# A focus attention kernel: later key groups four steps apart, their operations in another order on three engines

## The reference

```python
x = x + 0.5 * time_mix_ffn(layernorm(x))
x = x + causal_attention(layernorm(x))          # 16 heads of 8
x = x + 0.5 * time_mix_ffn(layernorm(x))
x = x + 0.5 * mixture(layernorm(x))             # 8 experts, top 2, hidden 256
x = x + focus(layernorm(x))
x = x + 0.5 * mixture(layernorm(x))
```

```python
kp = k_full @ lk_w.T + lk_b;  vp = v_full @ lv_w.T + lv_b
sk = ln(kp, lnd_w)                              # per head of 8
for i in range(3):
    sq = ln(qcur @ lq_w.T + lq_b, lnc_w) * rsqrt(temp)
    out = softmax(sq @ sk.T * INV_SQRT) @ vp
    diff = mean(abs(out - prev))                # decides on convergence
    qcur = qcur + out
output = out @ Wo.T + bo
```

## Time and profile before

| | |
|---|---|
| median of 3 runs | 1460.45 us (1457.98 to 1462.42) |
| the profiled execution | 1457.98 us, span 1456.2 us |
| PE busy | 1306.4 us (90%) |
| DVE busy | 1009.1 us (69%) |
| ACT busy | 869.7 us (60%) |
| POOL busy | 529.0 us (36%) |

### The profile page before, as it was taken

How to read it: one execution, slowest core, us unless ns; L and a number is a source line. 1 busy time by engine, 2 the same in 40 slices (tenths; PEclk the granted TensorE clock), 3 DMA queues, 4 the chain that set the end, 5 groups by cost and what they waited for, 6 DMA issues and landing times. The chain is left out here.

```text
span 1456.2 us, 36645 instructions
## 1 busy us (share of the span) xinstructions
PE 1306.4 (90%) x11651; PEld 920.2 (63%) x11651; DVE 1009.1 (69%) x3275; ACT 869.7 (60%) x1613; POOL 529.0 (36%) x818
## 2 busy tenths in 40 slices
PE   3699989989859999999999998999899998899998
PEld 2566766666636787776555555665555555577876
DVE  3688898898737873787677666767767666587444
ACT  3477777777524444434677777877677676333453
POOL 6366666665320320412233333343322321012444
PEclk9799999999969999999999999999999999899999
DMA  5322322322121012103445454555444442001332
GB/s 137 95 75 58 86 69 61 86 77 67 34 78 55 16 48 79 37 14 82 120 126 126 126 130 117 132 137 130 115 115 113 120 120 65 2 16 44 100 108 80
DMA packets 81070, 123.64 MB, mean 85 GB/s; under 512 B 10124, under 2 KB 64676, under 8 KB 71722
## 3 DMA queue, kind: packets, MB, share of 16 engines
q1 hardware_dynamic: 77866, 115.71, 30.7%
q0 software_dynamic: 3072, 6.30, 1.5%
HBM read 88.28 MB, written 33.56 MB: 84 GB/s over the span
## 5 line engine op out<-in xcount | busy, mean ns | idle before, releaser
L1417 ACT ACTIVATE e_buf<-ps_q 128x1024 f32<-128x1024 f32 x192 | 196.8, 1025 | 105.0 <-PE ps_q L2142 103.3
L2153 PE MATMUL ps_o<-e_buf,v_st 128*32 128x256 f32 x3072 | 209.5, 391 | 5.0 <-POOL v_st L1022 4.2
L1417 ACT ACTIVATE e_buf<-ps_k 128x1024 f32<-128x1024 f32 x192 | 196.0, 1021 | 19.6 <-PE ps_k L2142 19.5
L2003 PEld LDWEIGHTS ps_o<-w,e_buf 128*128 128x128 f32 x1280 | 152.2, 193 | 13.1 <-issue 12.0
L2003 PE MATMUL ps_o<-w,e_buf 128*128 128x128 f32 x1280 | 158.5, 277 | 0.0
L2591 DVE TENSOR_REDUCE mx<-ps_q 128x3 f32<-128x384 f32 x256 | 130.1, 548 | 27.4 <-PE ps_q L1707 26.8
L2142 PE MATMUL ps_q<-q_st,k_st 73*128 73x256 bf16 x768 | 118.5, 277 | 16.4 <-DMA q_st<-scr_q 13.2
L1234 ACT ACTIVATE e_buf<-ps_k 128x768 f32<-128x768 f32 x128 | 103.3, 807 | 47.3 <-PE ps_k L1718 45.4
L2153 PEld LDWEIGHTS ps_o<-e_buf,v_st 128*32 128x32 f32 x3072 | 81.3, 110 | 75.9 <-issue 36.8
L2142 PEld LDWEIGHTS ps_q<-q_st,k_st 73*128 73x128 bf16 x768 | 61.2, 98 | 96.8 <-issue 47.4
L3116 DVE COPY o_sb<-ps_o 128x256 f32<-128x256 f32 x192 | 80.0, 418 | 59.6 <-PE ps_o L2153 55.9
(11 more groups left out here) (403 smaller groups left out, 3063.5 us busy)
## 6 DMA issues: line engine op xcount, KB each, us to landing
q_st<-scr_q SPq DMA_DIRECT2D x64, 576.0 KB
k_st<-scr_k SPq DMA_DIRECT2D x192, 192.0 KB
scr_q<-parts SPq DMA_DIRECT2D x64, 192.0 KB, 2.9
scr_k<-parts SPq DMA_DIRECT2D x72, 64.0 KB
slots_in<-heads_out SPq DMA_DIRECT2D x3, 1536.0 KB
slots_out<-heads_out SPq DMA_DIRECT2D x18, 256.0 KB, 2.0
heads_out<-slots_in SPq DMA_DIRECT2D x15, 256.0 KB
out_dram<-x SPq DMA_DIRECT2D x8, 256.0 KB
```

The costliest lines, as they stand in the source:

```text
L1417: act.activation(e_buf[g % 2][:, hp * 2 % HG:hp * 2 % HG + 2, :], (ps_q, ps_k)[hp % 2][:, :, :], ACT.Exp).then_inc(sem("fast_exp"), 1)
L2003: last = mm(ps_o[:, e % 2, t * P:(t + 1) * P], h_sb[e % 2][:, f, t * P:(t + 1) * P], w2[:, e * NF + f, :], start=f == 0, stop=f == NF - 1)
L2153: last = mm(ps_o[VW * j:VW * j + VW, g % 2, 0:T], v_st[p][:, kt, HG * g + j, :], e_buf[g % 2][:, j, kt * T:(kt + 1) * T], start=kt == 0, s ...
```

## The change

The five pieces of a group start every four steps instead of every three. On TensorE the early value group of a late step is gone (order as in a plain step), and key_tokens is issued at hp 6 instead of at the end of the step. On VectorE key_queries and key_values come behind front_deviations and key_stats1, and key_norm2 comes behind the second evacuation. On SyncE the wait for the stores of the last group comes before fast_operands. The wait for the constants moves from inside the first mixture to ahead of it, on TensorE and VectorE.

```diff
-            return [(g, b - 3 * i) for i, g in enumerate(range(KEYS_LATE + 1, NG)) if 0 <= b - 3 * i <= 4]
+            return [(g, b - 4 * i) for i, g in enumerate(range(KEYS_LATE + 1, NG)) if 0 <= b - 4 * i <= 4]
...
 # SyncE
                         for g in late:
                             key_parts(g, late_parts)
+                            if g == NG - 1:
+                                sp.wait_ge(sem("K_out"), (g + 2) * 48 * GB)
                         if ahead:
                             fast_operands(*ahead, p, half + 1)
                         for g in late:
-                            sp.wait_ge(sem("K_out"), (g + 2) * 48 * GB)
+                            if g < NG - 1:
+                                sp.wait_ge(sem("K_out"), (g + 2) * 48 * GB)
...
 # TensorE, hp 3
-                                if late:
-                                    fast_values(n, p, 0)
                                 for g, step in late:
                                     if step == 1:
                                         pe.wait_ge(sem("K_hi"), g + 1)
...
                                 if not first:
                                     back_tokens(n - 1, b - 1, it, 0)
-                                if not late:
-                                    fast_values(n, p, 0)
+                                fast_values(n, p, 0)
...
 # TensorE, hp 6
-                                    if step in (2, 3):
+                                    if step in (1, 2, 3):
                                         pe.wait_ge(sem("fast_o_read"), (n - 1 + B) * NT + NT + 1)
+                                    if step == 1:
+                                        key_tokens(g)
...
 # TensorE, hp 7
                                 fast_values(n, p, 2)
-                                for g, step in late:
-                                    if step == 1:
-                                        pe.wait_ge(sem("fast_o_read"), (n - 1 + B) * NT + NT + 1)
-                                        key_tokens(g)
...
 # TensorE and VectorE, first mixture
-                    pe.wait_ge(sem("consts"), CONSTS + 8)
                     positions(k)
...
+            pe.wait_ge(sem("consts"), CONSTS + 8)
             for g in range(AHEAD):
                 mixture(g, g % 2, 0, True, more=lambda g, e: ahead(0, g, e))
...
 # VectorE, a step
                             evacuate_group(n - 1, NGV - 1)
-                        for g, step in late:
-                            if step == 2:
-                                key_queries(g)
-                            if step == 3:
-                                key_values(g)
                         if ahead:
                             front_deviations(ahead[0])
                         for g, step in late:
                             if step == 0:
                                 key_stats1(g)
+                        for g, step in late:
+                            if step == 2:
+                                key_queries(g)
+                        for g, step in late:
+                            if step == 3:
+                                key_values(g)
...
-                        for g, step in late:
-                            if step == 1:
-                                key_norm2(g)
                         evacuate_group(n, 1)
...
                                 key_norm1(g)
+                        for g, step in late:
+                            if step == 1:
+                                key_norm2(g)
```

More of the change, by code:

```diff
@@ L3580, in ahead @@
                 if (g, e) == (1, 1):
-                    dve.wait_ge(sem("consts"), CONSTS + 8)
                     tile_experts(k)
@@ L3636, in weigh_tiles @@
                 quad_out(CHUNKS[k][-1], QUADS - 1)
+            dve.wait_ge(sem("consts"), CONSTS + 8)
             for g in range(AHEAD):
```

## The result

The changed kernel took 1481.99 us as a median of four runs (1478.0 to 1485.28), the kernel before 1461.43 beside it, also of four. The ratio on record, 1.0165 with a 95% interval of 1.0131 to 1.02, is taken over all 34 executions of the changed kernel on record, and 1.65% of 1461 is 24 us; the two medians of four alone differ by 20.6. The direction was as forecast, the size not: 20.6 to 24 us slower where the forecast's sum had 12.0, and 1482 lies above the range's 1479. The profiled execution took 1485.11 us, 27 more than the one before.

What follows compares the result with a forecast made beforehand. The prediction took TensorE, busy 90% of the span, as the bound. Its terms summed to +12.0 us, giving 1470.0 from the profiled run and 1472.5 from the median, taken as 1471; range 1465 to 1477, widened to 1463 to 1479.

Steps and rivals of the forecast that it cites:

- Part 1: Groups start at steps 0, 4, 8: no work goes away, and moving piece 0 off the 15 us steps buys nothing.
- Part 2: TensorE in late steps, wait and transposes before the value product: −0.45 us where the wait is already met (pieces 0, 1, 4).
- Part 3: VectorE's order in pieces 2 and 3: TensorE waits uncovered; +1.6 us per piece 2 (+4.8), piece 3 at 15.4 (+1.1).
- Part 4: Piece 1, key_norm2 behind the second evacuation: TensorE waits 1.6 us, steps 5 and 9 last 11.8, step 1 stays.
- Part 5: Steps 4 and 8, pieces 4 and 0 together: 11.3 us, the next step 12.6, a pair 23.9.
- Part 6: SyncE's store wait before batch 14's key rows: +2.5 us, step 14 starting 23.5 us after step 12.
- Part 7: Constants wait ahead of the first mixture: TensorE's first product slips 1.7 us, taken as 0.6 in all; VectorE loses nothing.
- The sum: Steps 0 to 14 add up to 192.0 us against 180.58, +11.4; with the constants' 0.6, +12.0.
- the clock falls in the new gaps: Rival, 12%: five more stretches at the lower clock level, some 1.5 us each, add 7.5 to the forecast: 1479.

Runs made afterwards that it cites:

- e1: Kernel before with groups 5, 6, 7 four steps apart and SyncE's wait for the last group's stores ahead of its key rows: ratio 1.0046.
- e2: Kernel before with TensorE's order at hp 3 alone, wait and transposes ahead of value group 0 in every late step: ratio 0.9984.
- e7: Kernel before with only SyncE's wait for the last group's stores moved ahead of the same step's key rows, spacing 3: ratio 1.0020.
- e6: Kernel before with only the wait for the constants moved ahead of the first mixture: ratio 1.0011.
- after_again: The changed kernel unchanged, run on another chip: ratio 1.0145 to the kernel before.
- e10: Changed kernel with value group 0 issued once more, uncounted, ahead of the wait in steps with piece 2 or 3: ratio 1.0086 to the kernel before.
- e15: Kernel before with unread unit-matrix products added in three TensorE idle stretches, in steps 12, 16 and 32: ratio 0.9968.
- e16: Changed kernel with unread unit-matrix products added ahead of the wait of pieces 2 and 3 and ahead of step 14: ratio 1.0112 to the kernel before.

## Why the prediction was wrong

**Part 1 (spacing, no gain)** held: steps 0 to 11 of e1. Its reason was wrong in part: a piece 3 without piece 0 takes 13.93 for 14.5 with it, which step 9 had hidden with its low clock; the pairs take it back.

**Part 2 (−0.45)** can't be told from nothing by the times (e2), and by the steps it lies elsewhere: in e2 step 2 takes 11.53 for 12.09, while step 4 (10.58) is hardly shorter than the 10.67 before. Most of it is in pieces 2, not in the short steps.

**Part 3** held: 13.39 for 13.65, a wait of 1.70 for 2.0; piece 3 at full clock 15.26 for 15.4, its wait 1.70 where I had 1.4 to 1.8.

**Part 4** held: step 5 takes 12.30 for 12.6. key_norm2 took 1.54 for 1.68. Timeline after, step 5; the last transposes stand for 1.40:

```profile
754.35 0.38 PE L1633 MATMUL ps_m<-ident,y 128*128 128x128 f32 x2
...
756.13 0.63 PE L1633 MATMUL ps_m<-ident,y 128*128 128x128 f32 x4 [1.40 <-issue]
```

**Part 5** held: 11.26 and 12.30 for 11.3 and 12.6, a pair 23.6 to 24.4 for 23.9.

**Part 6** was 2 us short: step 14 starts 25.8 us after step 12, not 23.5. The stores were through 8.2 us behind the first issue, not 6.4 (816.1 + 2.9 makes 6.1, which the forecast took as 819.3): the landing of 2.9 that I took from the earlier trace rows belongs to another, single store. From the key rows to the start it took 11.9, not 11. The advice of the Trainium skill (DMA: Bandwidth & Descriptors, "Rules for kernel authors") to wait late agrees with e7, 3.1 us slower with the early wait alone.

**Part 7** held within what can be told: e6. The changed kernel's own profile can't show it, since there the stages ahead of the first mixture, which the change leaves alone, ended 4.3 us later than in the kernel before's. After, TensorE started 0.06 us behind the constant's end at 429.92 and VectorE 0.77 us, as far behind it as before. Timeline after, start of the first mixture:

```profile
429.63 0.29 POOL L773 TENSOR_SCALAR_AFFINE_SELECT k_const<-k_const 128x128 bf16<-128x128 bf16 x1
...
429.98 3.02 PE L1998 MATMUL ps_q<-z_t,w 128*128 128x512 f32 x3 [5.32 <-POOL k_const L773]
430.69 0.87 DVE L2526 BATCH_NORM_STATS2 st<-x 128x6 f32<-128x128 f32 x4 [4.78 <-POOL k_const L773]
```

**The sum** of steps 0 to 14, put together from rows at full clock: 11.5 + 11.7 (steps 0, 1), three times 13.39 and 15.26, twice 11.27 + 12.30, 10.6 + 15.1 (12, 13) and 9.8 make 191.8. The forecast said 192.0. Its parts erred by 2 us at most and against each other, so that the sum is this close is in part luck. Measured were 204.7: 12.9 us more, with 37.6 us at half clock. The second profile, after_again, gives 12.4 with 30.4. The kernel before has a share of its own in its 180.7: e6, with the same orders and no low stretch, takes 177.3, some 3.3 less. So of the 24.1 us between the two profiles about 14.5 are waits and 9.6 clock, an estimate from these sums.

So the step that failed is none of the seven; it is the sum, which added them as if idle stretches of TensorE cost their length, with nothing for the clock behind them. The rival "the clock falls in the new gaps" had the mechanism, but stood with 12% as something else than the forecast, where it had to lie on top: of the waits of 1.3 us or more in the changed kernel's trace, twelve in all (pieces 2 and 3 six times, piece 1 three times, the pairs twice, step 14), all were in my own forecast. And its size was too small: five stretches of 1.5 us, 7.5, for 12.9. Laid on top, 12.9 us give 1484 for the 1482 measured.

My doubt about it was that step 6 kept 1.00 with the same gaps as steps 3 and 9. That was read rightly, but it says only that the fall is not certain. Timeline of TensorE before, in step 3:

```profile
719.69 0.61 PE L2142 MATMUL ps_q<-q_st,k_st 73*128 73x256 bf16 x4 [0.67 <-ACT e_buf L1417]
721.07 0.71 PE L2125 MATMUL ps_m<-block_w,y_t 128*128 128x128 f32 x4 [0.77 <-DVE y_t L3093]
...
722.15 1.86 PE L2153 MATMUL ps_o<-e_buf,v_st 128*32 128x256 f32 x16
```

Two idle stretches of 0.67 and 0.77 us stand ahead of the value product at the lower level, in step 9 as well; step 6 has both and keeps the clock. So a piece-3 step could lose the clock without any long wait, as it did in 7 of 30; with the uncovered wait behind the two short ones it did in 12 of 12. The Trainium skill (TensorE: Matmul & The Clock Gate, "What's actually happening") says that activity releases the throttle. The trace agrees in the mean: e10, e15 and e16 add activity alone, and the time at the lower level falls from 37.6 and 30.4 us to 17.2 and 6.9 in e10 and e16, and to none around the filled waits of e15.

Two things stay open. How many us of the loss belong to the clock is known from step sums of single profiles (12.9, or 9.6 beside the kernel before) and from e10 and e16 (9, and 5 to 8 us), not from one clean run. And in the kernel before itself the low stretches come and go: 6.7 us in its profile, none in e6's, 10.1 in steps 3, 6 and 9 of e7, which are as before there; which run gets them was not settled.

## What to carry to other kernels

Price an uncovered wait of TensorE at more than its length: here twelve of them, 1.3 to 5.3 us long, cost on average another 1.1 us each in work at half clock (12.9 over 12, an estimate from one profile), most of it where short gaps stood ahead of the wait. Two reorderings that cost little or nothing alone can be most of the loss together, when each relies on the other's cover; test them in pairs. Where a wait can't be removed, products that nobody reads can fill it; they must not outlast the wait (e16 lost 2.5 us that way), and they do not always keep the clock up (steps 3 and 7 of e10, step 11 of e16).

## What the runs showed of the hardware

TensorE's granted clock fell to the lower level around idle stretches of 1.4 to 5.3 us inside dense work, not each time, and also behind two short ones of 0.67 and 0.77 us. With three waits filled, and no fall by chance elsewhere, the three iterations of e15_warm ran at full clock. Busy time of one stretch, 700 to 1250 us, which is nearly all of them: e15_warm, then e7_sync_wait on a chip where the kernel before takes as long:

```profile
700.00:1250.00 550.00, 512.61 (x5615) 326.86 (x5616) 380.38 (x1139) 406.31 (x508) 182.07 (x329) 1.00 0.47 121
```

```profile
700.00:1250.00 550.00, 506.59 (x5445) 317.57 (x5448) 376.05 (x1119) 400.08 (x501) 181.57 (x329) 0.98 0.48 120
```

The chips differ: with the same work, the stage behind the focus block had a granted clock of 0.97 on the chip of the kernel before's profile and 0.86 in e15_warm on another. Busy time by stage, first the kernel before, then e15_warm, most of the second mixture:

```profile
1240.00:1456.00 216.00, 200.45 (x1269) 154.19 (x1268) 121.25 (x484) 88.39 (x200) 61.61 (x64) 0.97 0.19 59
```

```profile
1255.00:1529.00 274.00, 219.98 (x1270) 169.16 (x1270) 120.60 (x485) 87.42 (x200) 61.04 (x64) 0.86 0.15 47
```

It takes 58 us longer there, of which 19.5 are TensorE's busy time; the rest is idle time that was not looked into. A time of one chip must not be set against that of another.
